# Merging the stages behind the layers of a graph-network kernel

## The reference

```python
x = x + L0(h)                    # three attention layers over the edges; log_softmax at the end

def L1(feat, src, dst):          # ten power steps
    deg = segment_sum(ones, dst)
    norm = clip(deg, 1) ** -0.5
    h = feat
    for _ in range(10):
        h = 0.9 * segment_sum((h * norm)[src], dst) * norm + 0.1 * feat
    return h

def L2(x, edge_attr, weight, bias):
    dis = rsqrt(out_degree + 1)
    msg = (dis[row] * dis[col]) * (concat(x[row], edge_attr) @ weight)
    return segment_sum(msg, col) + bias

def L3(feats, src, dst, W, attn_l, attn_r, bias):
    z = leaky_relu(feats) @ W
    e = leaky_relu((z @ attn_l)[src] + (z @ attn_r)[dst])
    alpha = segment_softmax(e, dst)
    return segment_sum(alpha * z[src], dst) + bias

# around each: h = relu(layernorm(x)); x = x + Lk(h, ...)
```

## Time and profile before

| | us |
|---|---|
| median of three runs | 4897.83 |
| lowest, highest | 4896.31, 4903.46 |
| the profiled execution, its own time | 4912.25 |
| its span | 4910.5 |
| PE busy in the span | 3513.1 (72%) |
| DVE | 3256.5 (66%) |
| POOL | 2498.9 (51%) |
| ACT | 2423.5 (49%) |

### The profile page before, as it was taken

How to read it: one execution, slowest core, us unless ns; L and a number is a source line. 1 busy time by engine, 2 the same in 40 slices (tenths; PEclk the granted TensorE clock), 3 DMA queues, 4 the chain that set the end, 5 groups by cost and what they waited for, 6 DMA issues and landing times. The chain is left out here.

```text
span 4910.5 us, 91838 instructions
## 1 busy us (share of the span) xinstructions
PE 3513.1 (72%) x24220; PEld 3047.3 (62%) x24220; DVE 3256.5 (66%) x10240; ACT 2423.5 (49%) x8504; POOL 2498.9 (51%) x2591
## 2 busy tenths in 40 slices
PE   3677766666667666666657778777846999964887
PEld 2555555555555555555546667777746999962787
DVE  7677776777567776777737777777763333324996
ACT  0766666665376666666456666665421000000554
POOL 5777777674477777777267777777511000000000
PEclk9777888998578888988757888888757999975555
DMA  3444444442334444444144444444222000000001
GB/s 78 101 102 105 101 119 117 118 123 72 84 92 101 103 112 116 119 118 121 35 105 98 101 98 104 105 106 101 65 81 104 2 2 2 1 21 7 2 3 23
DMA packets 596225, 389.26 MB, mean 79 GB/s; under 512 B 441290, under 2 KB 518210, under 8 KB 595720
## 3 DMA queue, kind: packets, MB, share of 16 engines
q1 hardware_dynamic: 392839, 156.12, 12.5%
q0 software_dynamic: 81344, 84.68, 9.9%
q10 hardware_dynamic: 121536, 142.57, 9.8%
HBM read 315.36 MB, written 67.70 MB: 78 GB/s over the span
## 5 line engine op out<-in xcount | busy, mean ns | idle before, releaser
L615 POOL DMA_INDIRECT arena<-node_table,arena x1660 | 1603.2, 966 | 612.6 <-issue 467.8
L770 PE MATMUL ps<-arena 128*128 128x129 f32 x4980 | 948.3, 321 | 184.6 <-DVE arena L920 102.0
L679 ACT ACTIVATE arena<-arena 128x129 f32<-128x129 f32 x2490 | 742.8, 301 | 456.9 <-DVE arena L888 452.1
L770 PEld LDWEIGHTS ps<-arena 128*128 128x128 f32 x4980 | 791.0, 226 | 270.9 <-DVE arena L920 137.0
L917 DVE TENSOR_SCALAR arena<-arena 128x128 f32<-128x128 uint16 x2490 | 883.2, 360 | 94.7 <-PE ps L770 41.8
L615 POOL DMA_INDIRECT arena<-last_node_table,arena x830 | 794.1, 957 | 290.0 <-issue 233.5
L888 DVE TENSOR_TENSOR arena<-ps,arena 128x258 f32<-128x258 f32 x1245 | 524.3, 421 | 590.0 <-PE ps L759 247.9
L1165 PE MATMUL ps<-arena 128*128 128x192 bf16 x6875 | 589.6, 247 | 56.0 <-PEq L86 40.3
L1165 PEld LDWEIGHTS ps<-arena 128*128 128x128 bf16 x6875 | 587.4, 98 | 58.1 <-issue 52.3
L759 PE MATMUL ps<-arena,e 128*128 x2484 | 498.4, 332 | 113.4 <-DVE arena L888 56.5
L759 PE MATMUL ps<-arena 128*128 x2496 | 499.4, 333 | 103.6 <-ACT e L669 33.0
(11 more groups left out here) (324 smaller groups left out, 4705.8 us busy)
## 6 DMA issues: line engine op xcount, KB each, us to landing
arena<-in_attr SPq DMA_DIRECT2D x1245, 96.0 KB, 2.3
arena<-slot_rows ACTq DMA_DIRECT2D x249, 320.0 KB
edge_counts<-al ACTq DMA_DIRECT2D x397, 100.0 KB
arena<-node_table,arena POOLq DMA_INDIRECT x1660
edge_counts<-stage ACTq DMA_DIRECT2D x198, 100.0 KB
arena<-last_node_table,arena POOLq DMA_INDIRECT x830
arena<-edge_counts SPq DMA_DIRECT2D x24, 500.0 KB
stage<-edge_counts SPq DMA_DIRECT2D x16, 500.0 KB, 5.4
```

Source lines behind the costliest of these rows:

```text
L615: pool.indirect_dma_start(out=RING[:, t % R_SLOTS, XO:XO + XG], out_offset=None, in_=table[:, :], in_offset=bass.IndirectOffsetOnAxis(ap=I ...
L679: ins = act.activation(PR[j % 3][:, q], PR[j % 3][:, q], ACT.Copy, accum_out=AL[w % 2][:, c:c + 1])
L770: ins = pe.matmul(BPS[j % 2][:, 0:AB], WOH[j % 2][:, q], RING[:, r + q, D32:D32 + AB], start=q == 0, stop=q == BT - 1)
```

## The change

1. `phase` clears runs of neighbouring semaphores with one instruction each.
2. The in-degree matmuls move into the stage of the layout of counts: the PE follows the chunks as they are laid.
3. Power steps, norm, L2 and L3 projections become one stage of 28 semaphores. Four loop trips of two power steps stay; the last two steps and the L2 matmuls are written out. In the last step the DVE does residual, norm and split per group of five blocks. The residual stays in SBUF (`XS`, in `stage`) from there to the end of the kernel.
4. L2's sums and edge features are turned and projected together (96 rows). Projections, norm and the L3 projections run per group, the engines one group apart. The left attention part is a 65th column of W, made by a small product at the stage's start, as is the right part; both need both attention vectors and the transposed W.
5. `divide` adds the chunk to the residual, POOL adds the L3 bias beforehand, SP stores each chunk to `out`. The last stage and the `attended` table go.

The core of the diff:

```diff
@@ phase
-        for s in sems.values():
-            nc.gpsimd.sem_clear(s)
+        nums = sorted(s.num for s in sems.values())
+        at = [k for k in range(len(nums)) if not k or nums[k] != nums[k - 1] + 1] + [len(nums)]
+        for k in range(len(at) - 1):
+            nc.gpsimd.sem_clear(range(nums[at[k]], nums[at[k + 1] - 1] + 1))
@@ layout of counts
+            @block.tensor
+            def _(pe):
+                pe.wait_ge(s["one"], 1)
+                k = 0
+                for d in range(NB):
+                    while k < NCK and k * CW_ * WIN < (d + 1) * P:
+                        pe.wait_ge(laid[k % NST], k // NST + 1)
+                        k += 1
+                    for sx in range(NB):
+                        pe.matmul(ps[:, 3072 + d:3073 + d], adj3[:, sx, d * P:(d + 1) * P], ONEB, start=sx == 0, stop=sx == NB - 1)
@@ the merged stage, SP: XS (800 KB), W2, W3E, two attention vectors, B2
@@ PE
+                pe.wait_ge(s["ld"], 80)
+                pe.transpose(ps[0:D, 3584:3584 + D], W3E[0:D, 0:D], identf[0:D, 0:D]).then_inc(s["w3t"], 1)
+                pe.wait_ge(s["w3c"], 1)
+                pe.wait_ge(s["alr"], 1)
+                pe.matmul(ps[0:D, 3584 + P:3584 + 2 * P + 1], SQ[0:D, 0], WT[0:D, :], start=True, stop=True).then_inc(s["wlr"], 1)
...
+                with pe.Fori(0, STEPS // 2 - 1) as i:
+                    for k in range(2):
+                        power(i, k)
+                for k in range(2):
+                    power(STEPS // 2 - 1, k)
+                power(STEPS // 2, 0)
...
+                turn_sums(0)
+                pe.wait_ge(s["pm"], NS + 7)
+                for i in range(6):
+                    if i < 4:
+                        turn_sums(i + 1)
+                    if i:
+                        turn_nodes(i - 1)
+                    if i < 5:
+                        project_sums(i)
+                    if i:
+                        project_nodes(i - 1)
@@ DVE
-                st.link(dve.tensor_tensor(G, R, bc(VEC(2)), ALU.mult))
+                for q in range(5):
+                    b = slice(5 * q, 5 * q + 5)
+                    st.link(dve.tensor_tensor(G[:, b], R[:, b], bc(VEC(2)[:, b]), ALU.mult))
+                    st.link(split3(dve, st, G[:, b], G3[0][:, b]))
+                    dve.sem_inc(s["g0"], 1)
                 st.link(dve.tensor_scalar(C0, G, TELE, None, ALU.mult))
...
+                dve.wait_ge(s["ld"], 80)
+                st.link(dve.tensor_copy(WT[0:D, 0:P], ALR[0:D, 1:2].to_broadcast([D, P])))
+                dve.tensor_copy(WT[0:D, P:P + 1], ALR[0:D, 0:1]).then_inc(s["alr"], 1)
+                dve.wait_ge(s["wlr"], 1)
...
+                for d in range(5):
+                    power(STEPS // 2 - 1, 1, d)
+                    b, v = slice(5 * d, 5 * d + 5), SS[d % 2]
+                    st.link(dve.tensor_tensor(G[:, b], G[:, b], bc(VEC(1)[:, b]), ALU.mult))
+                    st.link(dve.tensor_tensor(XS[:, b], XS[:, b], G[:, b], ALU.add))
+                    spread_of(XS[:, b], G[:, b], v)
+                    dve.wait_ge(s["std"], d + 1)
+                    st.link(dve.reciprocal(v[:, 1], v[:, 1]))
+                    st.link(dve.tensor_tensor(G[:, b], G[:, b], bc(v[:, 1]), ALU.mult))
+                    st.link(dve.scalar_tensor_tensor(G[:, b], G[:, b], 0.0, bc(DIS[:, b]), ALU.max, ALU.mult))
+                    st.link(split3(dve, st, G[:, b], G3[0][:, b]))
+                    dve.sem_inc(s["g0"], 1)
...
+                def add_sums(i):
+                    b, y, v = slice(5 * i, 5 * i + 5), YH[i % 2], SS[i % 2]
+                    dve.wait_ge(s["po"], i + 1)
+                    if i >= 2:
+                        dve.wait_ge(s["ht"], i - 1)
+                    st.link(dve.tensor_tensor(y, P2P, bc(DIS[:, b]), ALU.mult))
+                    dve.sem_inc(s["pr"], 1)
+                    st.link(dve.tensor_tensor(XS[:, b], XS[:, b], y, ALU.add))
+                    spread_of(XS[:, b], y, v)
+                    dve.wait_ge(s["std"], 5 + i + 1)
+                    st.link(dve.reciprocal(v[:, 1], v[:, 1]))
+                    st.link(dve.tensor_tensor(y, y, bc(v[:, 1]), ALU.mult))
+                    st.link(dve.tensor_scalar(y, y, 0.0, None, ALU.max))
+                    dve.scalar_tensor_tensor(y, y, 0.2, y, ALU.mult, ALU.max).then_inc(s["hn"], 1)
...
+                for i in range(6):
+                    if i < 5:
+                        add_sums(i)
+                    if i:
+                        copy_projected(i - 1)
@@ attention
+            @block.gpsimd
+            def _(pool):
+                pool.wait_ge(s["bl"], 16)
+                pool.tensor_tensor(XS, XS, B3.unsqueeze(1).to_broadcast([P, NB, D]), ALU.add).then_inc(s["b3"], 1)
...
-                    if i:
-                        dve.wait_ge(s["wr"], 16 * i)
...
-                    dve.tensor_tensor(OUTC, out_v[:, :, 0:D], bc(OC), ALU.mult).then_inc(s["oc"], 1)
+                    st.link(dve.tensor_tensor(OUTC, out_v[:, :, 0:D], bc(OC), ALU.mult))
+                    dve.wait_ge(s["b3"], 1)
+                    dve.tensor_tensor(XS[:, b], XS[:, b], OUTC, ALU.add).then_inc(s["oc"], 1)
```

More of the change, by code:

```diff
@@ L1127, in _ @@
                 st = Steps(dve, s["st"])
+                dve.memset(ONEB, 1.0).then_inc(s["one"], 1)
                 st.link(dve.tensor_reduce(VEC(0), R, AX.X, ALU.max))
@@ L1172, in summed, with _ @@
                 .rearrange("p c (a b) -> p c b a", a=3)
[L1174 to L1193, removed]
+        names = "rt rtd g0 ps pm st xl ld alr w3t w3c wlr wx att tt tc po pr var std hn ht hc z er zc erc"
+        with phase(nc, names) as (block, s):
+            NS = STEPS * 5
+            @block.sync
+            def _(sp):
+                sp.dma_start(XS, blk(res_t)).then_inc(s["xl"], 16)
+                sp.dma_start(W2[0:DE, :], a["L2_gnn_weight"]).then_inc(s["ld"], 16)
+                sp.dma_start(W3E[0:D, 0:D], a["L3_gnn_W"]).then_inc(s["ld"], 16)
+                sp.dma_start(ALR[0:D, 0:1], a["L3_gnn_attn_l"].rearrange("(n o) -> n o", o=1)).then_inc(s["ld"], 16)
+                sp.dma_start(ALR[0:D, 1:2], a["L3_gnn_attn_r"].rearrange("(n o) -> n o", o=1)).then_inc(s["ld"], 16)
+                sp.dma_start(B2, a["L2_gnn_bias"].rearrange("(o n) -> o n", o=1).to_broadcast([P, D])).then_inc(s["ld"], 16)
             @block.scalar
@@ L1198, in _ @@
                 act.activation(VEC(1), VEC(0), ACT.Sqrt).then_inc(s["rtd"], 1)
+                act.wait_ge(s["w3t"], 1)
+                act.activation(SQ[0:D, 0], ps[0:D, 3584:3584 + D], ACT.Copy).then_inc(s["w3c"], 1)
+                for i in range(5):
+                    act.wait_ge(s["var"], i + 1)
+                    act.activation(SS[i % 2][:, 1], SS[i % 2][:, 1], ACT.Sqrt).then_inc(s["std"], 1)
+                act.wait_ge(s["ps"], NS)
+                act.activation(SE[:, :, D:DE], e32[:, :, :], ACT.Copy).then_inc(s["att"], 1)
@@ L1402, in build @@
-        gat_t = nc.dram_tensor("attended", (NP, D), f32).ap()
+                            step(i, k, d)
+                    st.leave_body()
+                st.leave(STEPS // 2 - 1)
+                for d in range(5):
+                    step(STEPS // 2 - 1, 0, d)
+                dve.wait_ge(s["xl"], 16)
+                for d in range(5):
+                    power(STEPS // 2 - 1, 1, d)
[9 more added lines that the diff above has]
+                    dve.sem_inc(s["g0"], 1)
@@ new lines, in copy_projected @@
+                def copy_projected(i):
+                    dve.wait_ge(s["z"], i + 1)
+                    dve.tensor_copy(Z[:, 5 * i:5 * i + 5, 0:D], ZP[:, :, 0:D])
+                    dve.tensor_copy(EL[:, 5 * i:5 * i + 5], ZP[:, :, D]).then_inc(s["zc"], 1)
+                for i in range(6):
+                    if i < 5:
+                        add_sums(i)
+                    if i:
+                        copy_projected(i - 1)
+        FB = N // P
+        B3 = stage[:, 1600:1600 + D]
```

305 lines of the change are left out of this document (118 added, 187 removed).

## The result

The kernel as changed takes **4735.1 us** (median of 4 runs, 4730.04 to 4745.82), the kernel before 4900.65 us beside it (4 runs, 4896.31 to 4906.09): ratio 0.9662, 95% interval 0.9643 to 0.9681. The forecast was 4730 (4706 to 4758). The two profiled executions lie 14.4 and 3.9 us above the medians of their kernels, so the spans differ by more than the medians, which are 165.6 us apart.

A forecast was written before the change was run, and what follows sets the result against it. PE bounds the power steps, DVE attention; between them no engine holds the time. Terms sum to -167.5 us, 4744.75 for the profiled execution; the difference applied to the median 4897.83 gives 4730 us, range 4706 to 4758.

The forecast's parts named there:

- Clears: Borders behind setup and layers: 326 fewer clears at 0.075 us, a range priced as one single clear; -24.5 us.
- a range is cleared one by one: Rival at the borders: range clears cost per semaphore what single clears do, no gain, +26 us, 4756 us; chance 0.12.
- The layers' -6.9 us: Layers ahead of the changed stages: forecast to keep their work, only borders change; 0 us.
- In-degrees: 625 one-column matmuls go under the layout of counts, at no cost to its length; -17.0 us, its border another -1.4.
- Start of the power steps: Merged stage's start: PE waits for `alr`, first power matmul 16.9 us behind the DVE's first operation instead of 6.4; +10.5 us.
- Power steps and norm: Three loop turns stay, -3.7 us; norm on the DVE hidden under the last power step, stall of 1.1 us, -40.7 us.
- Node stages: L2 and L3 node stages overlap by group, 9.0 us each, 53.8 us with border in place of 129.6; -75.8 us.
- The rival with the rising clock: Rival in the node stages: PE clock rises, loop takes 7.45 us, about 9 us go, 4721 us; chance 0.15.
- Attention: Attention stage: residual additions in `divide` +2.1 us, POOL's bias addition meeting the DVE +2.7 us.
- The DVE meets it in its first maxima: Attention's start: POOL's bias addition begins some 3.3 us in and reaches into the DVE's maxima; +2.7 us, bounds 0 and 3.7.
- End: Kernel's end: last stage goes, two small stores and 3.5 us behind them, 4.4 us in place of 24.1; -19.7 us.

The follow-up runs named there:

- a_alr: Changed kernel with the small product of W and the attention vectors moved to around the ninth power step; 5734.22 us, ratio 0.9706 to the kernel before.
- a_extra4: Changed kernel with four more DVE operations of 320 elements per group under the last power step; in all +7.9 us, groups 11.55 us apart.
- a_again: The changed kernel once more, unedited, beside the experiments; 5798.75 us, ratio 0.9734 to the kernel before.
- a_best: Changed kernel with small product moved, all ten power steps written out, bias addition moved out of attention; 5765.5 us, ratio 0.9684 to the kernel before.
- a_degend: Changed kernel with all 625 in-degree matmuls waiting for the layout's last chunk; merged stage begins 18.47 us behind ACT's last copy, 2.34 in the changed kernel.
- a_noadd: Changed kernel without the residual addition in `divide`, so the output lacks it; attention 374.14 us, against 376.27 in a trace where POOL began alike.
- a_clears5: Changed kernel with each range clear issued five times; four more clears cost 0.89 us with 30 semaphores, 2.38 and 2.31 with 100.

## Why the prediction was right, step by step

*Clears: right in kind, 2.5 us too much.* Two prices were off: 0.075 us for a single clear was 0.071 (330 of them, 1.3 us), and 0.075 for a range was 0.22 and three times 0.585 (1.7 us). That makes -21.5 where the rows have -22.0. Of the rival "a range is cleared one by one" so much is true that the cost grows with the number of semaphores, by 0.0052 us each, a fourteenth of a single clear; its 26 us of loss did not come. The Trainium skill (Runtime: NRT & Kernel Launch, The ~15µs preamble/postamble breakdown) would have given, as an estimate, 0.03 us and kept 10 us; the traces kept 2.

*The layers' -6.9 us* has no cause in the change that I can name. It has the size of the scatter: the execution profiled before lay 10.5 us further above its median than the one after, and the first layer, from its first operation to the last one ahead of the next border, took 1496.3 to 1520.3 us in the eleven traces of the experiments, which all have one text there.

*In-degrees: 1.8 us too much with the clears of this border.* Behind ACT's last copy 17.7 us went (20.08 before, 2.34 after), nearly what was forecast; the tail of one block was 0.88 us (0.7 at most had been allowed). What the forecast put at nothing is the layout's own length with matmuls beneath it: 1.1 us more in this pair, 0.6 to 4.4 over the others.

*Start of the power steps: right to 0.3 us.* Each named operation stands where it was put. It was a cost that the stage did not have to pay: a_alr takes 13.1 us off the start by moving one wait, and gives 0.8 back later, since nothing up to the L2 step needs the product.

*Power steps and norm: right* to 0.2 us each: 9.5 us of DVE work under 10.555 us of PE, a stall of 1.01 (1.1 forecast), no clock drop. a_extra4 shows how near the edge it was.

*Node stages: 2.8 us too long.* The loop was put at 9.05 us a group and measured 8.7 to 8.9, and 7.9 for the one group at the upper clock: 2.0 us together. (The terms given for the loop add up to 9.2 and not 9.0, those of the tail to 7.5 and not 7.6.) The start came 0.6 us sooner (3.2, not 3.8), since the clock had not fallen yet, where the forecast had it low; the last group and the tail 0.2. The rival with the rising clock came true for one group of five in this execution and for none in a_again, a_best and a_degend (granted clock 0.56, stage 52.0 us); the 0.60 here are that group and the first 6.9 us.

*Attention: right in size; the place differs from one execution to the next.* "The DVE meets it in its first maxima", at 2.7 us, is what five of the nine traces show (2.6 to 2.7 at the 25th maximum, attention 375.8 to 376.0 us). In the four others, the profile above among them, POOL began 3.07 us into the stage or sooner, and not 3.3, and met the last small operation ahead of the maxima for its full length, 3.26 us here. Both are exclusion: the maximum ran its own 0.7 us behind POOL's end, and sharing could not stretch 0.30 us to 3.55. For the maximum, which has two SBUF inputs, the trace now agrees with the Trainium skill (SBUF — State Buffer, SBUF: two separate sides); L1551 has one array and two scalars, and was held all the same. The additions were 2.1 us as forecast, by a_noadd.

*End: 1.1 us too little.* From the last DVE operation to the span's end are 3.3 us, issues included; I had put 3.5 behind the issues.

*The sum.* Without the layers' 6.9 us the terms come to 166.4 us where 167.5 had been forecast, but this is partly luck: clears, layout, start and attention came out 5.2 us dearer than forecast, node stages, power steps and end 4.1 us cheaper. The mechanisms are right term by term; no single size was off by over 3 us.

## What to carry to other kernels

When a stage is merged into the one before it, list what its first instruction on the bounding engine waits for: here one small product ahead of the loop held the PE for 13 us, and it could stand anywhere up to the tenth step. Work laid under a bounding engine costs nothing visible up to the length of that engine's group, and behind this point its excess for each group and, once the PE stalls for long, the clock too; read the idle time ahead of the covered engine's first operation to see how much is left. Work of an idle engine laid beside transfers is not quite free: here the layout grew by some 2 us. Where an operation lasts exactly as long as one on another engine that began just before it, look at what the two share, not at the operation.

## What the runs showed of the hardware that I had not expected

- A range of semaphores is cleared for about 0.067 us and 0.0052 us for each semaphore in it (a_clears5); one by one they cost 0.071 us each.
- The layout of counts takes 64.3 to 65.6 us alone and 66.2 to 68.7 with 625 small matmuls beneath it.
- A DVE operation of 0.9 or 0.3 us that meets POOL's of 3.55 is held until that one ends; a MEMSET is not (a_again).
- One turn of the loop on PE costs 2.3 to 4.4 us over the group's 10.555, in the same place from one execution to the next: 2.5 us without a matmul ahead of 3822.03, the rest at the lower clock. In the two places of a_best and a_alr where a small product stands between the groups, 0.28 and 0.55 us.
- The PE kept its upper clock over a stall of 1.01 us and had lost it behind one of 7.17 us (0.18 us a matmul in place of 0.084).
- The same program takes 4735 us in the first measurement and 5799 in a_again, and the difference is in the layers alone. It shows in waits for transfers and for what hangs on them: in the changed kernel's first profile the gathers (L617) never waited for a load of `in_attr` (it lands in 2.2 us at the median); in a_again they stood 217.2 us for it, 111.7 for `slot_rows`, and 795 us for buffers that the PE frees, in place of 92. Why the loads land later there no run shows.
